# A two-layer recurrent kernel: the conditions' products in two scaled 16-bit halves, and x's first chunk loaded in four pieces

## The reference

```python
# layer 0: x (64, 128, 512), h0 = cond (64, 512)
f = sigmoid(x @ W_f.T + b_f);  i = sigmoid(x @ W_i.T + b_i);  s = f + i + EPS
new_info = i / s * (x @ W_h.T + b_h)
L = cumsum(log(f / s + EPS), axis=1)
scaling = exp(L[:, -1:] - padded(L)[:, :-1])
x1 = x + cumsum(scaling * new_info, axis=1) + exp(L) * cond[:, None]
# layer 1: a gated recurrence over t with the conditions v
vz, vr, vh = cond @ C_z + b_z, cond @ C_r + b_r, cond @ C + b
z = sigmoid(x1_t @ W_z + h @ U_z + vz);  r = sigmoid(x1_t @ W_r + h @ U_r + vr)
hh = tanh(x1_t @ W + (r * h) @ U + vh);  h = (1 - z) * h + z * hh
out = x1 + all h
```

## Time and profile before

| | |
|---|---|
| Median of three runs | 1522.3 us (1522.21 to 1522.66) |
| The profiled execution's own time | 1523.06 us |
| Its span (first to last instruction) | 1521.2 us |
| PE (matmuls) busy | 1509.1 us, 99% |
| DVE busy | 1317.1 us, 87% |
| ACT busy | 1061.2 us, 70% |
| POOL busy | 304.1 us, 20% |

### The profile page before, as it was taken

One profiled execution on the slowest core, in us unless ns is written; L12 is line 12 of the kernel. 1 busy time (PEld: TensorE's weight loads), 2 busy tenths in 40 slices (PEclk: granted clock), 3 DMA queues, 4 the chain that ended last, 5 costly groups with the idle time before them and its releaser, 6 DMA issues.

```text
span 1521.2 us, 57907 instructions
## 1 busy us (share of the span) xinstructions
PE 1509.1 (99%) x24654; PEld 1184.8 (78%) x24654; DVE 1317.1 (87%) x2894; ACT 1061.2 (70%) x2472; POOL 304.1 (20%) x329
## 2 busy tenths in 40 slices
...
PEclk9999999999999999999999999999999999999999
...
GB/s 197 28 150 209 85 147 177 120 165 136 174 107 120 123 136 99 82 44 30 48 21 48 48 20 48 29 39 48 21 48 48 21 48 21 48 41 3 32 31 31
DMA packets 544162, 116.85 MB, mean 77 GB/s; under 512 B 520096, under 2 KB 526496, under 8 KB 535200
## 3 DMA queue, kind: packets, MB, share of 16 engines
...
...
## 4 chain that ended last, share of the span: by engine, by line
PE 98%; DVE 1%; DMA 0%; issue 0%; ACT 0%; SPq 0%; DVEq 0%
PE ps L1392 33%; PE ps L1494 23%; PE ps L1457 22%; PE ps L1506 12%; PE ps L1478 6%; PE ps L1410 2%; PE ps L1359 1%; DMA raw<-in_x 0%; PE ps L1423 0%; DVE ST L1237 0%; DVE AR L1204 0%; DVE RL L1272 0%; DVE HL L1316 0%; ACT ST L841 0%; DVE ST L1323 0%
## 5 line engine op out<-in xcount | busy, mean ns | idle before, releaser
L1392 PE MATMUL ps<-XH,WH 128*128 128x512 f16 x1872 | 404.7, 379 | 0.0
L1392 PEld LDWEIGHTS ps<-XH,WH 128*128 128x128 f16 x1872 | 183.1, 98 | 220.2 <-issue 0.3
L1494 PE MATMUL ps<-HL,U 128*128 128x64 f16 x8016 | 275.3, 193 | 1.8 <-DVE HL L1316 1.7
L1494 PEld LDWEIGHTS ps<-HL,U 128*128 128x128 f16 x8016 | 259.1, 98 | 8.2 <-issue 3.1
L1605 POOL TENSOR_TENSOR ST<-ST 128x256 f32<-128x256 f32 x127 | 107.7, 848 | 460.9 <-ACT ST L834 460.9
L812 ACT ACTIVATE ST<-ST 128x128 f32<-128x128 f32 x254 | 72.0, 310 | 170.2 <-DVE ST L1237 170.0
L1506 PE MATMUL ps<-HL,U 128*128 128x64 f16 x4064 | 163.1, 194 | 0.0
L1237 DVE SCALAR_TENSOR_TENSOR ST<-ps,dn,AR 128x128 f32<-128x128 f32 (+1 forms) x320 | 108.6, 372 | 46.8 <-PE ps L1506 44.1
L1237 DVE SCALAR_TENSOR_TENSOR ST<-ps,dn,XP 128x128 f32<-128x128 f32 x315 | 107.4, 372 | 40.6 <-PE ps L1506 38.1
L1506 PEld LDWEIGHTS ps<-HL,U 128*128 128x128 f16 x4064 | 138.6, 98 | 0.1
L1494 PEld LDWEIGHTS ps<-RL,U 128*128 128x128 f16 x3952 | 131.8, 98 | 6.1 <-issue 1.0
...
## 6 DMA issues: line engine op xcount, KB each, us to landing
...
```

The source lines that it names most:

```text
L1392: op = pe.matmul(ps[b][:, :], v[:, g, wp, k, e * P:(e + 1) * P], y[:, xp, k, :], start=n == 0, stop=n == 11)
L1494: pe.matmul(ps[b][:, col:col + B], U[:, g, uh, k, e * P:(e + 1) * P], S[:, k, 0], start=opens, stop=False, skip_group_check=True)
```

## The change

The conditions' weights and `cond` are split into scaled 16-bit halves, as the other operands are. One condition's weights at a time are loaded into CF (at pairs 6, 12 and 16); DVE finds their largest magnitude (`c_largest`, at the end of pairs 7, 12, 16), POOL reduces it over the partitions, DVE derives the scale (pairs 9, 13, 17), ACT writes the high halves (`c_high`, end of pairs 9, 13, 17) and DVE the low halves (`c_low`, end of pairs 10, 14, 18). CT is scaled and split once in pair 7 (`conditions`). `condition` now makes 48 matmuls of 64 columns in 16 bit, at the head of pairs 13, 17 and 21, and `add_b2` also multiplies by the scale back. At the start, chunk 0 of x comes from a second input array in four contiguous pieces, one for each k, W_f's first half in two pieces of 128 columns, and PE runs 10 matmuls on zeros in place of 14. At the end one semaphore counts the last stores where there were three.

```diff
@@ -30,7 +30,7 @@
 PARTS = TC // 2
-WARM = 14
+WARM = 10
 JOINT = TC
@@ -80,7 +80,11 @@
         U = over("U", w_at + 24576, 12288, F16).rearrange("p (g h k n) -> p g h k n", g=3, h=2, k=KT)
-        CW = over("CW", w_at + 24576, 6144).rearrange("p (g k n) -> p g k n", g=3, k=KT)
+        CF = over("CF", w_at + 32768, 2048)
+        CW = over("CW", w_at + 40960, 4096, F16).rearrange("p (h k n) -> p h k n", h=2, k=KT)
+        CS = AR[:, 11776:12032].bitcast(F16).rearrange("p (h k b) -> p h k b", h=2, k=KT)
         XB = [a.rearrange("p (h k n) -> p h k n", h=2, k=KT) for a in (stage[1].bitcast(F16), over("XB1", xs_at + 16384, 4096, F16))]
@@ -153,13 +159,22 @@
-        def half256(a, half):
-            return a[:, :, half * 256:(half + 1) * 256]
-        W1_ORDER = [(g, half) for half in range(2) for g in range(3)]
+        W1_PIECES = [(0, 0, 1), (0, 1, 1), (1, 0, 2), (2, 0, 2), (0, 2, 2), (1, 2, 2), (2, 2, 2)]
+        def w1_piece(a, i):
+            g, e, n = W1_PIECES[i]
+            return a[:, :, e * P:(e + n) * P]
+        def w1_made(g, e):
+            begins = [piece[0:2] for piece in W1_PIECES]
+            return begins.index((g, e)) + 1 if (g, e) in begins else None
         C_ORDER = (1, 2, 0)
         C_STAGE = {1: CR, 2: CH, 0: CZ}
-        C_PAIR = {2 * WIDE + 2: 1, 2 * WIDE + 3: 2, 2 * WIDE + 4: 0}
+        C_PAIR = {13: 1, 17: 2, 21: 0}
+        C_LARGEST, C_SCALE, C_HIGH, C_LOW = {7: 0, 12: 1, 16: 2}, {9: 0, 13: 1, 17: 2}, {9: 0, 13: 1, 17: 2}, {10: 0, 14: 1, 18: 2}
         W2_ORDER = (1, 0, 2)
@@ -176,7 +191,8 @@
             return ([W1S + 2, W1S] if q == 1 else [W1S + 1] if q == 2 else []) + ([r] if s == 1 else []) \
-                + ([XS0 + c] if q % 2 and WIDE <= c < NCH else []) + ([X1] if q == NQ - 4 else [])
+                + ([XS0 + c] if q % 2 and WIDE <= c < NCH else []) + ([X1] if q == NQ - 4 else []) \
+                + ([CS0] if q == 7 else []) + ([CS0 + 1 + C_SCALE[q]] if q in C_SCALE else [])
@@ -457,18 +475,19 @@
             def load_w1(i):
-                g, half = W1_ORDER[i]
-                sp.dma_start(half256(stage_k(g), half), half256(by_k(staged[g]), half)).then_inc(d_w1[i], 16)
+                g = W1_PIECES[i][0]
+                sp.dma_start(w1_piece(stage_k(g), i), w1_piece(by_k(staged[g]), i)).then_inc(d_w1[i], 16)
...
             load_w1(0)
-            for i, k in enumerate((0, 2)):
-                sp.dma_start(xbuf[0][:, k * 512:(k + 2) * 512], x[0][:, k * 512:(k + 2) * 512]).then_inc(d_x0[i], 16)
+            for k in range(KT):
+                sp.dma_start(xbuf[0][:, k * 512:(k + 1) * 512], x0[k]).then_inc(d_x0[k], 16)
             load_w1(1)
+            load_w1(2)
             sp.dma_start(B1, b1).then_inc(d_b1, 16)
-            for i in range(2, 6):
+            for i in range(3, len(W1_PIECES)):
                 load_w1(i)
@@ -487,17 +506,20 @@
-                    sp.wait_ge(*((s_xlo, c) if c else (s_x0lo, 2)))
+                    sp.wait_ge(*((s_xlo, c) if c else (s_x0lo, KT)))
                     sp.wait_ge(s_maxx, c + 1)
...
                     load_stage(SPLIT[q - 4])
-                if q == 2 * WIDE:
-                    sp.wait_ge(s_mm[2], 4 * WIDE)
-                    for g in C_ORDER:
-                        sp.dma_start(CW[:, g], by_k(staged[C_STAGE[g]])).then_inc(d_stage[C_STAGE[g]], 16)
+                n = {2 * WIDE: 0, 12: 1, 16: 2}.get(q)
+                if n is not None:
+                    if n:
+                        sp.wait_ge(s_clo, 2 * n + 1)
+                    else:
+                        sp.wait_ge(s_mm[2], 4 * WIDE)
+                    sp.dma_start(CF, staged[C_STAGE[C_ORDER[n]]]).then_inc(d_cw, 16)
                 r = split_turn(q - 4)[0]
@@ -597,15 +618,24 @@
                 act.wait_ge(d_stage[SPLIT[r]], 16)
-                if r >= 3:
-                    act.wait_ge(s_cmm, 3)
+                if r >= 4:
+                    act.wait_ge(s_clo if r == 4 else s_cmm, 7 if r == 4 else 3)
                 act.activation(split_place(r)[:, 0], stage_k(SPLIT[r]), ACT.Abs, accum_out=mx[:, scale(r)]).then_inc(s_maxw, 1)
...
                 act.activation(split_place(r)[:, 0, k], stage_k(SPLIT[r])[:, k], ACT.Copy, scale=up[:, scale(r)]).then_inc(s_shi, 1)
+            def c_high(n):
+                act.wait_ge(s_up, scaled(CS0 + 1 + n))
+                if n:
+                    act.wait_ge(s_cmm, n)
+                for half in range(2):
+                    k = slice(2 * half, 2 * half + 2)
+                    act.activation(CW[:, 0, k], by_k(CF)[:, k], ACT.Copy, scale=up[:, scale(CS0 + 1 + n)]).then_inc(s_chi, 1)
@@ -1003,12 +1037,15 @@
                 dve.tensor_scalar(up[:, c], er[:, c], 2.0 / least, 2.0 ** 13 / room, ALU.min, ALU.mult).then_inc(s_up, 1)
-                if i >= XS0:
+                if XS0 <= i < CS0:
...
                     dve.tensor_scalar(bx[:, i - XS0], B1[:, 2], up[:, scale(W1S + 2)], up[:, c], ALU.mult, ALU.mult).then_inc(s_bx, 1)
+                if i > CS0:
+                    dve.wait_ge(s_dn, n)
+                    dve.tensor_scalar(dc[:, i - CS0 - 1:i - CS0], dn[:, c], dn[:, scale(CS0)], None, ALU.mult).then_inc(s_dc, 1)
                 if i == X1:
@@ -1083,12 +1120,34 @@
+            def conditions():
+                dve.wait_ge(s_up, scaled(CS0))
+                dve.tensor_scalar(CS[:, 0], CT, up[:, scale(CS0)], None, ALU.mult).then_inc(s_chi, 1)
+                dve.wait_ge(s_chi, 1)
+                dve.scalar_tensor_tensor(out=CS[:, 1], in0=CT, scalar=up[:, scale(CS0)], in1=CS[:, 0],
+                                         op0=ALU.mult, op1=ALU.subtract).then_inc(s_clo, 1)
+            def c_largest(n):
+                dve.wait_ge(d_cw, 16 * (n + 1))
+                dve.tensor_reduce(mx[:, scale(CS0 + 1 + n)], CF, AX.X, ALU.max, apply_absolute_value=True).then_inc(s_maxc, 1)
+            def c_low(n):
+                for half in range(2):
+                    k = slice(2 * half, 2 * half + 2)
+                    dve.wait_ge(s_chi, 2 * n + half + 2)
+                    dve.scalar_tensor_tensor(out=CW[:, 1, k], in0=by_k(CF)[:, k], scalar=up[:, scale(CS0 + 1 + n)],
+                                             in1=CW[:, 0, k], op0=ALU.mult, op1=ALU.subtract).then_inc(s_clo, 1)
             def add_b2(g):
-                if g == C_ORDER[0]:
+                n = C_ORDER.index(g)
+                if n == 0:
                     dve.wait_ge(d_b2, 16)
-                dve.wait_ge(s_cmm, C_ORDER.index(g) + 1)
+                dve.wait_ge(s_cmm, n + 1)
+                dve.wait_ge(s_dc, n + 1)
                 for e in range(KT):
-                    op = dve.tensor_scalar(V[:, g, e], ps[bank("v", g)][:, e * B:(e + 1) * B], B2[:, g, e:e + 1], None, ALU.add)
+                    op = dve.tensor_scalar(V[:, g, e], ps[bank("v", g)][:, e * B:(e + 1) * B], dc[:, n:n + 1], B2[:, g, e:e + 1],
+                                           ALU.mult, ALU.add)
                     if e == KT - 1:
@@ -1102,6 +1161,8 @@
                     exponent(i)
+                    if i == CS0:
+                        conditions()
                 gates(q)
@@ -1123,6 +1184,10 @@
                     x_largest(c + 2)
+                if q in C_LOW:
+                    c_low(C_LOW[q])
+                if q in C_LARGEST:
+                    c_largest(C_LARGEST[q])
@@ -1349,15 +1414,15 @@
             def condition(g):
-                b, n = bank("v", g), C_STAGE[g]
-                s = CW[:, g]
-                pe.wait_ge(d_cond, 16)
-                pe.wait_ge(d_stage[n], 16)
+                b, n = bank("v", g), C_ORDER.index(g)
+                pe.wait_ge(s_chi, 2 * n + 3)
+                pe.wait_ge(s_clo, 2 * n + 3)
                 wait_bank(pe, "v", g)
                 for e in range(KT):
-                    for k in range(KT):
-                        op = pe.matmul(ps[b][:, e * B:(e + 1) * B], s[:, k, e * P:(e + 1) * P], CT[:, k, :],
-                                       start=k == 0, stop=k == KT - 1)
+                    for i in range(12):
+                        (wp, cp), k = PRODUCTS[i // KT], i % KT
+                        op = pe.matmul(ps[b][:, e * B:(e + 1) * B], CW[:, wp, k, e * P:(e + 1) * P], CS[:, cp, k],
+                                       start=i == 0, stop=i == 11)
                 op.then_inc(s_cmm, 1)
@@ -1375,15 +1440,15 @@
                                 pe.wait_ge(s_w1xlo, W1_SPLIT.index(g) + 1)
-                        if c == 0 and a == 0:
+                        if c == 0 and w1_made(g, e) is not None:
                             if n == 0:
-                                pe.wait_ge(s_w1hi, 3 * h + g + 1)
+                                pe.wait_ge(s_w1hi, w1_made(g, e))
                             if n == KT:
-                                pe.wait_ge(s_w1lo, 3 * h + g + 1)
-                        if q == 0 and i == 0 and n in (0, 2):
-                            pe.wait_ge(s_x0hi, n // 2 + 1)
```

(21 more changed lines are left out.)

41 lines of the change are left out of this document (23 added, 18 removed).

## The result

The changed kernel takes 1525.25 us (median of 20 runs, 1522.45 to 1526.7), the kernel before 1522.82 us beside it (20 runs, 1521.26 to 1524.0). The ratio is 1.0014, with an interval of 1.0008 to 1.0020: 2.1 us slower, between 1.2 and 3.0. That is less than the 0.2% (3 us) that I had set as the line between "same" and "slower", with the upper end of the interval on that line. The profiled execution took 1522.82 us (span 1521.0), 2.4 us less than the median of its kernel's runs; that of before took 1523.06. It is one of four of the 20 that lie between 1522.45 and 1522.82; the other sixteen lie between 1524.0 and 1526.7.

What follows compares the result with a forecast made beforehand. PE, busy for 99% of the span, bounds the kernel, with DVE and ACT close behind. Conditions -6.4, waits +8.1 and start -1.6 sum to +0.1 us, giving 1522.4 us, range 1514.0 to 1527.5.

Steps and rivals of the forecast that it cites:

- Part 1, the conditions: Conditions' matmuls on PE: three of 3.52 us become 144 16-bit matmuls in 4.20 us, a gain of 6.36 us.
- Part 2, the ring: DVE and ACT, passing work back and forth, need 67.1 us per four pairs, PE 63.56; PE waits 8.1 us.
- the three named: PE's predicted waits for x_lo: 1.3 us in pair 12, 3.4 in pair 16, 3.4 in pair 20.
- Rival (a): Pairs 7 to 18: DVE has room for the added 16 us; 1514.3 us, faster; chance 0.30.
- Rival (b): Pairs 16 and 20: PE's waits bring the clock down, 3.4 us on top; 1525.8 us, slower; chance 0.25.
- The third wait of 3.4 us: PE's predicted wait for x_lo in pair 20, part of the 8.1 us in all.
- Part 3, the start: Start: smaller pieces of x and W1F let PE's fourth matmul begin at 8.9 us, not 10.55; gain 1.6 us.
- The slow stretch: PE at 1.2 GHz after its two idle gaps at the start, costing 1.7 us; left unchanged, bounds -1.7 and +1.7.
- CF's loads: Loads of 1 MB at pairs 6, 12, 16, waiting in SP behind the store of x1; taken as nothing.
- the forecast: First stage: PE waits of 6 to 10 us with the clock untouched, range 1519.5 to 1525.5 us; chance 0.45.

Runs made afterwards that it cites:

- 3, c_low in the gap: The changed kernel with c_low moved ahead of hidden in the same pairs (10, 14, 18): 1519.75 us, ratio 0.9975 to the kernel before.
- run 5: The changed kernel with PE making one group of 12 matmuls twice in pairs 11, 15 and 19: 1524.83 us, ratio 1.0012 to the kernel before.
- run 9: Run 7 with c_largest(2) at the end of pair 19 instead of in pair 20, its CF load two pairs sooner: 1514.53 us, ratio 0.9944.
- Run 2: The kernel before with only the changed kernel's new start: 1520.75 us, ratio 0.9983 to the kernel before.
- run 1: The changed kernel without its new start (14 warm matmuls, x in two pieces, W1F in halves): 1528.13 us, ratio 1.0034 to the kernel before.
- 4, c_low on POOL: The changed kernel with c_low made by POOL after its HB addition in pairs 8, 12, 16, not by DVE: 1532.41 us, ratio 1.0057.
- 6, spread: The changed kernel with c_low ahead of hidden and the second and third conditions' steps spread over later pairs: 1516.46 us, ratio 0.9954.
- 7, with the warm matmuls: Run 6 with 14 matmuls on zeros at the start in place of 10: 1515.56 us, ratio 0.9949 to the kernel before.

## Why the prediction came out, step by step

- **Part 1, the conditions: right.** 48 matmuls take 1.40 us in the chain, 2.12 us less than the 3.52 of the earlier trace rows; three times that is the 6.36 us of the sum.
- **Part 2, the ring: right.** Each leg came within 0.3 us, the cycle at 67.2 for 67.1, the places were the three named. Runs 3 and 5 show that it is the ring that counts: thinning a leg takes the time away, work on PE doesn't add any. The sum was 8.6 us for the predicted 8.1, as 1.7 + 3.44 + 3.5, and 9.2 by the length of the f16 part. Rival (a) held for the earlier trace rows as totals, and not for the order: the same total fits without a wait in run 9.
- **Rival (b), right in its sign and wrong in its price.** My forecast had the clock untouched, and that didn't hold: the granted clock did fall behind a wait of 3.4 us, as it did at the start. The Trainium skill's rule (TensorE: Matmul & The Clock Gate, Part 1) that the clock is taken down once PE has been idle agrees with that here. But I wrote that a slow stretch doesn't let DVE catch up, since gates(16) waits for x_lo and ACT, and charged 3.4 us on top. Its reason is also why it costs nothing: if gates(16) waits for x_lo and ACT and not for PE, the ring goes on at its 67.2 us, and PE, being late, finds x_lo(10) ready sooner. The third wait of 3.4 us, which I had priced at pair 20, was the cover. I had charged the same microseconds twice. The time of (b), 1525.8 us, lies nearer to the measured 1525.25 than my 1522.4 does. The clock behind these waits isn't what brings the time there: the f16 part is 2.8 to 3.0 us longer than before whether the clock took 1.6 us, 2.9 or, in run 5, nothing.
- **Part 3, the start: under-sized.** I took 1.6 us. In the profile of after the fourth matmul starts at 8.14 us, where I had 8.9; before it starts at 10.67 us, where I had 10.55. That is 2.5 us. Run 2 measures 2.6 us (1.2 to 4.0) for the new start as a difference of medians. The slow stretch, which I left as it was, wasn't there in the profiled execution, so the f16 part begins at 105.56 us, 4.0 us sooner than before. With the new start and ten warm matmuls there are eight profiles. In them the fourth matmul starts between 8.0 and 9.7 us, and the matmuls from there to the f16 part take 97.4 us (three profiles), 1.4 to 1.6 us more (four) or 2.6 us more (one).
- **CF's loads** cost nothing that a row shows, as taken.

Three stretches give the account of each profile against that of before: the start (when the f16 part begins; before 109.55 us), the f16 part (before 414.60), and the rest from the second stage on (before 997.1), in which no line of code differs but the semaphore of the last stores. All in us:

| kernel | start | f16 part | rest | whole span | all executions, by the ratio |
|---|---|---|---|---|---|
| after | -4.0 | 417.45 (+2.85) | +0.9 | -0.2 | +2.1 (1.2 to 3.0) |
| after, second profile | -4.2 | 417.57 (+2.97) | +0.1 | -1.0 | |
| after, third profile | -3.7 | 417.40 (+2.80) | +0.5 | -0.4 | |
| 1, conditions alone | -0.5 | 417.39 (+2.79) | +2.6 | +4.9 | +5.2 (3.5 to 7.0) |
| 2, new start alone | -0.8 | 414.60 (0) | -0.1 | -1.0 | -2.6 (-4.0 to -1.2) |
| 3, c_low in the gap | -2.4 | 412.69 (-1.91) | +0.1 | -4.2 | -3.8 (-5.2 to -2.4) |
| 4, c_low on POOL | -2.1 | 423.25 (+8.65) | +0.2 | +6.7 | +8.7 (6.7 to 10.5) |
| 5, more work for PE | -0.5 | 417.43 (+2.83) | +0.1 | +2.5 | +1.8 (0.5 to 3.2) |
| 6, spread | -2.2 | 409.66 (-4.94) | +0.6 | -6.6 | -7.0 (-9.0 to -5.2) |
| 7, with the warm matmuls | -3.2 | 409.69 (-4.91) | +0.1 | -8.0 | -7.8 (-9.6 to -5.8) |
| 9, the best | -3.4 | 408.46 (-6.14) | +0.8 | -8.7 | -8.5 (-10.5 to -6.4) |

(Last column: the ratio less one, by 1523 us. On POOL the lost clock is 4.4 us: 15.59 and 16.79 us for 64 matmuls behind waits of 3.8 and 3.9.)

The middle column is the change's own mechanism. It repeats within 0.2 us in the five profiles with after's order of DVE's work, however they start and whatever the clock takes. The sum of the steps gives it to within 0.5 us: -6.36 for the conditions, plus the waits and the lost clock, plus 0.17 for each wait. For after that is -6.36 + 8.61 + 0.5 = +2.75 for the measured +2.85, for the best -6.36 for -6.14. My forecast for it was -6.4 + 8.1 = +1.7.

The outer columns are the noise of this kernel. The start moved by up to 3.6 us between profiles with the new start, and the rest by 0.8 us between the three profiles of the changed kernel, in steps of 0.1 to 0.4 us at different places, and by 2.6 us in run 1. No record names a cause for the latter. **Open** is therefore what the sixteen executions near 1525 us have more than the three profiled ones, which took 1522.0 to 1522.8 us. A start as in runs 3 to 5 would give 1.6 to 3.5 us of it, and a rest as in run 1 1.7 us or more; both are of the right size. Run 2 fits the first: its eleven times fall into groups at 1519.1 to 1519.4, 1520.7 to 1521.3 and 1522.1 to 1522.2 us, spaced like the starts in the profiles. But no profile was taken of such an execution of the changed kernel, so this is not shown.

In total, the prediction of 1522.4 us against 1525.25 holds within its range, for the reason of the forecast (waits of 6 to 10 us that eat the conditions' gain). How near it came is in part luck. In the profiled execution the start gained 2.4 us more than I took, the f16 part cost 1.1 us more and the rest 0.9 us more, which nearly cancels: -0.2 us for the forecast +0.1. And the median lies 2.4 us above that execution, for which the sum has no term.
